# From the fourth norm to the third attention: one stage of 64 batches instead of five stages in a row

## Chip, cores, metric

One core of a Trainium2 chip runs the whole program. The metric is the device time in microseconds (us) of one execution; lower is better.

## What is computed

Eight layers act on x, 32 batches of 128 tokens with 128 features (4,096 rows). Each adds its result to x after a layer norm. The change touches layers five to seven, and the weighted addition that ends layer four:

```
x = x + _L1_ffn_ref(_layernorm(x), ...)                         # experts, two rows per token come back
x = x + _L2_xattn_ref(_layernorm(x), ctx_1024, ctx_1024, L2_xattn_w_concat)
x = x + _L2_ffn_ref(_layernorm(x), L2_ffn_weight, L2_ffn_bias)  # values rounded to float8, one 128x128 product
x = x + _L3_xattn_ref(_layernorm(x), ctx_1024, ctx_1024, L3_xattn_Wq, L3_xattn_Wk, L3_xattn_Wv, L3_xattn_Wo)

def _L2_xattn_ref(query, key, value, w_concat):      # 16 heads of 8 features
    scores = einsum('bhqd,bhkd->bhqk', q, k) / sqrt(d_k)
    ctx = einsum('bhqk,bhkd->bhqd', softmax(scores), v)
    return ctx @ w_concat.T
```

The third attention is the same with its queries, keys and values first projected by Wq, Wk and Wv. Batches do not mix: what happens to one batch of x depends on that batch and its context alone.

## The kernel before

x lies in on-chip memory as `k.X`, 32 tiles of 128 tokens by 128 features. Four tiles are a chunk (CHUNKS = 8). The program is a row of stages, each a block of its own: all engines meet at its end, and the next one begins with its memsets and loads. The stages in question are called in `network` as

```
        norm_phase(k, "n4", routed=2)
        softmax_phase(k, "a2", w_o=a["L2x_Wo"], ctx_tok=a["ctx_tok"])
        norm_phase(k, "n5", quant=(a["L2f_wT"], a["L2f_b"]))
        norm_phase(k, "n6", add_y=True)
        softmax_phase(k, "a3", *(a[f"L3x_W{w}"] for w in "qkvo"))
```

`norm_phase` (L238) works on all 32 tiles in passes. VectorE (DVE) adds the returned expert rows (L234) or the transposed result of the float8 layer (L432), takes the statistics of every tile (L442, L448), and only then are all reciprocal roots made at once (ScalarE, ACT, L338; DVE L458). DVE normalises (L468), TensorE (PE) transposes four tiles into one PSUM bank (L386), ACT copies that out (L349, L352), and DVE subtracts to get the low part (L485), so that each float32 value is held as a high and a low part. In n5 the same pass rounds to float8 and multiplies by the quantised weights (L400); n6 turns the result back (L372) and adds it.

`softmax_phase` (L2155) then treats the 32 batches one by one, a batch being an item. The queue of SyncE (SP) writes queries and keys of a chunk to DRAM (L2285, L2297) and reads them back in the layout in which four heads share a product: twelve transfers of 32 KB per two batches into `ring` (L2318), three of 256 KB per chunk into `stat` (L2331). For one item PE makes four score products (`scores`, L2423); DVE takes the row maxima of each (`top`, L2599), splits them in two parts (L2607, L2609); PE turns them (L2430), ACT puts them under the queries (`keep_max`, L2538); PE makes the shifted, transposed scores (`shifted`, L2439), ACT the exponentials (`curve`, L2545), PE the products with the values (`times_v`, L2454); the result is taken out (L2550), turned (L2464), divided (DVE L2616, L2619), turned again (L2469), multiplied by the output weights (L2473) and added to X (`add`, L2625). The order of the instructions on each engine is written out by hand in its `item`: scores of the next item, the second half of the values of the last one and its ending lie between the shifted groups of this one. There are two PSUM banks for scores and two for shifted scores, so the third score product waits for the maxima of the first. GpSimd (POOL) spreads the values of each item into `select` (L2387), two copies per item.

In a3 each item also has one of four pieces of a chunk ahead of it (`next_piece`): three 512-column products for values, keys or queries (L115 to L117, `mm3`), or the transposes of the values (L2406); POOL splits keys and queries (L2367, L2369).

## Time and profile before

| | us |
|---|---|
| device time, three runs | 2375.51, 2400.9, 2409.84 (median 2400.9) |
| profiled execution: its span | 2426.7 |
| n4, from the end of the last experts' products to a2's first instruction | 1280 to 1333 |
| a2: until its first score, then 32 items | 1333 to 1350.5, to 1581 |
| n5, n6 | 1581 to 1651.5 |
| a3: until its first score, then 32 items | 1651.5 to 1682.4, to 1902 |

The profiled execution has no time of its own beside the span, which counts from its first instruction to its last. PE is busy 1647.8 us of it (68%), DVE 1160.6, ACT 964.2, POOL 833.2. In the rows further on, times are us from the start of the span unless marked ns; PEclk is TensorE's granted clock as a share of 2.4 GHz, so 0.50 means 1.2 GHz. A busy PE is not PE at its peak: its matmuls overlap, and at the lower clock the same ones take longer.

### The profile page before, as it was taken

The page shows a single profiled execution, that of the slowest core. Times are in us where ns is not written, and L with a number is a line of the kernel's source. Part 1 is how long each engine was busy: PE and PEld are TensorE (multiplying, and loading weights), DVE is VectorE, ACT ScalarE, POOL GpSimd, SP SyncE. Part 2 cuts the span into 40 slices and gives each one's busy share as a digit, 9 for nine tenths or more (in the row PEclk, how much of TensorE's full clock was granted, in tenths as well). Part 3 has the DMA queues.
Part 4 walks back from the last instruction along what each step waited for, and adds up shares of the span by engine and source line. Part 5 has one row for each costly group of instructions (what it writes and reads, how often), then busy time and mean ns, then how long its engine had stood idle before and what let it go on. Part 6 is the DMA issues. An engine that isn't in the chain of part 4 may idle for free. (4 is left out here: it accounts for less than half of the span.)

```text
span 2426.7 us, 39580 instructions
## 1 busy us (share of the span) xinstructions
PE 1647.8 (68%) x10584; PEld 1305.3 (54%) x10584; DVE 1160.6 (48%) x3507; ACT 964.2 (40%) x2129; POOL 833.2 (34%) x994
## 2 busy tenths in 40 slices
PE   2009933989924888610991799935999626888883
PEld 2009933779913777610991577723777514555552
DVE  3302247542265777630226446675466584334463
ACT  0004412743314887400441435625466313454541
POOL 1364523855514111037450100002112047714447
PEclk9999975999956999755995558955699658999996
DMA  5727840227622333021322524202243032534432
GB/s 158 276 64 207 233 122 17 92 73 216 201 78 79 95 89 91 3 70 60 102 60 76 139 71 109 66 2 78 71 119 87 5 141 69 145 102 121 123 92 62
DMA packets 210383, 246.40 MB, mean 102 GB/s; under 512 B 36064, under 2 KB 168416, under 8 KB 208800
## 3 DMA queue, kind: packets, MB, share of 16 engines
q1 hardware_dynamic: 188832, 199.16, 29.2%
q0 software_dynamic: 21376, 45.13, 5.7%
q8 instruction: 83, 1.36, 0.2%
q14 instruction: 92, 0.75, 0.1%
HBM read 150.09 MB, written 94.10 MB: 101 GB/s over the span
## 5 line engine op out<-in xcount | busy, mean ns | idle before, releaser
L912 POOL DMA_INDIRECT out_rows<-m_yr,ids x220 | 211.2, 960 | 235.2 <-DVE ids L1096 190.1
L1039 ACT ACTIVATE m_hf<-m_psu,m_b 128x256 f32<-128x256 f32 x284 | 116.7, 470 | 361.8 <-PE m_psu L981 361.8
L524 POOL DMA_INDIRECT in_rows<-Y,sent_to x192 | 207.0, 1078 | 149.0 <-issue 57.6
L2599 DVE TENSOR_REDUCE a_mx<-a_pss 128x4 f32<-128x512 f32 x256 | 170.2, 686 | 127.8 <-PE a_pss L2423 127.7
L994 PEld LDWEIGHTS m_psy<-m_raw,m_hf 128*128 128x128 f32 x1760 | 213.4, 192 | 5.4
L981 PE MATMUL m_psu<-m_xt,m_raw 128*128 128x256 f32 x880 | 213.8, 387 | 1.8 <-DVE m_xt L1085 1.2
L994 PE MATMUL m_psy<-m_raw,m_hf 128*128 128x128 f32 x1760 | 213.8, 275 | 0.0
L2439 PEld LDWEIGHTS a_psx<-a_stat,a_ring 128*128 128x128 f32 x1024 | 182.1, 234 | 20.8 <-issue 9.4
L968 PE MATMUL m_pst<-ident,select 128*128 128x128 f32 x220 | 44.0, 283 | 205.3 <-DMA select<-in_rows 203.4
L2439 PE MATMUL a_psx<-a_stat,a_ring 128*128 128x128 f32 x1024 | 183.3, 310 | 0.1
L2545 ACT ACTIVATE Y<-a_psx 128x512 f32<-128x512 f32 x256 | 151.5, 597 | 75.6 <-PE a_psx L2439 66.7
L1306 POOL DMA_INDIRECT m_got<-out_rows,sent_to x128 | 123.8, 967 | 165.0 <-DMA out_rows<-m_yr 88.7
L981 PEld LDWEIGHTS m_psu<-m_xt,m_raw 128*128 128x128 f32 x880 | 162.5, 195 | 21.0 <-issue 2.9
L2387 POOL COPY select<-a_vx 128x64 f32<-128x64 f32 x128 | 30.2, 237 | 380.1 <-PE a_pso L2454 377.8
L1296 POOL DMA_INDIRECT in_rows<-Y,sent_to x128 | 128.2, 1001 | 63.7 <-issue 38.7
L2423 PE MATMUL a_pss<-a_ring,a_stat 96*128 96x512 f32 x256 | 128.4, 547 | 31.3 <-DMA a_stat<-stat_rows 30.3
L1586 DVE TENSOR_TENSOR m_hrow<-m_curved,m_psa 128x128 f32<-128x128 f32 x192 | 55.4, 288 | 183.9 <-ACT m_curved L1447 183.1
L968 PEld LDWEIGHTS m_pst<-ident,select 128*128 128x128 f32 x220 | 28.4, 147 | 208.6 <-DMA select<-in_rows 205.1
L1085 DVE COPY m_xt<-m_pst 128x256 f32<-128x256 f32 x110 | 45.7, 416 | 195.9 <-PE m_pst L968 195.9
L1919 PE MATMUL a_pso<-Y,select 128*128 128x128 f32 x1024 | 136.9, 280 | 0.0
L1919 PEld LDWEIGHTS a_pso<-Y,select 128*128 128x128 f32 x1024 | 133.1, 197 | 2.6
L1375 PE MATMUL m_psa<-m_experts,m_xt 128*128 x384 | 120.8, 397 | 0.6 <-ACT m_xt L1442 0.6
(330 smaller groups left out, 3549.7 us busy)
## 6 DMA issues: line engine op xcount, KB each, us to landing
m_raw<-in_L0f_w SPq DMA_DIRECT2D x41, 512.0 KB, 3.6
m_raw<-in_L0x_w SPq DMA_DIRECT2D x39, 512.0 KB
a_ring<-mov_rows SPq DMA_DIRECT2D x576, 32.0 KB
a_stat<-stat_rows SPq DMA_DIRECT2D x72, 256.0 KB, 4.2
in_rows<-xn SPq DMA_DIRECT2D x7, 2448.0 KB, 32.9
select<-in_rows SPq DMA_DIRECT2D x110, 136.0 KB
n_got<-out_rows SPq DMA_DIRECT2D x24, 512.0 KB, 4.1
m_xr<-in_rows SPq DMA_DIRECT2D x96, 128.0 KB
```

The lines of the kernel that those rows point to most:

```text
L524: pool.indirect_dma_start(k.in_rows[:], bass.IndirectOffsetOnAxis(ap=k.sent_to[:, j, i:i + 1], axis=0), rows[:, i], None).then_inc(sem, 16)
L912: pool.indirect_dma_start(k.out_rows[:], bass.IndirectOffsetOnAxis(ap=k.ids[:, n:n + 1], axis=0), yr[:, b % OUT, i], None).then_inc(y_out[ ...
L981: last = pe.matmul(psu[b % 2][:, f * B:f * B + B], raw[:, n % RAW, f * D:f * D + D], xt[:, b % 2], start=True, stop=True)
L994: last = pe.matmul(psy[b % 2][:, D * i:D * i + D], hf[:, b % 2, f * B + D * i:f * B + D * i + D], raw[:, v, UP + f * D:UP + f * D + D], st ...
L1296: pool.indirect_dma_start(k.in_rows[:], bass.IndirectOffsetOnAxis(ap=k.sent_to[:, j, i:i + 1], axis=0), k.rows[:, i], None).then_inc(sent[ ...
L1306: pool.indirect_dma_start(got[:, g % GOT], None, k.out_rows[:(h + 1) * NT * D], bass.IndirectOffsetOnAxis(ap=k.sent_to[:, j, i:i + 1], axi ...
L1375: pe.matmul(psg[n % 2], xt[:, n % 2], wres[:, bass.ds(expert[n] * WC, UP)], start=True, stop=True) \
L1919: last = pe.matmul(pso[j % 2][:, D * o:D * o + D], window, prob[:, j % 2, g, D * (h % 4):D * (h % 4) + D], start=r == 0, stop=r == OCT - 1)
L2423: pe.matmul(pss[g % 2][:], stat[:ROWS, u, g, b * D:b * D + D], ring[:ROWS, s, g, :, D * (b % 2):D * (b % 2) + D], start=True, stop=True).t ...
L2439: last = pe.matmul(psx[g % 2][:, D * h:D * h + D], ring[:, s, g, h, D * (b % 2):D * (b % 2) + D], stat[:, u, g, b * D:b * D + D], start=Tr ...
L2545: act.activation(prob[:, j % 2, g], psx[g % 2][:], ACT.Exp, scale=scale).then_inc(probs.sem, 1)
L2599: dve.tensor_reduce(mx[:, j % 2, 4 * g:4 * g + 4], pss[g % 2][:].rearrange("p (h q) -> p h q", h=4), AX.X, ALU.max).then_inc(maxed.sem, 1)
```

## The change

The five stages become one block, `stream_phase`, of 64 items: item n is batch n of the second attention for n below 32, and batch n - 32 of the third from 32 on. What the norms did in passes is done per chunk, at fixed places between the items, by a class `ChunkNorm` with three instances: `before` (norm in front of the second attention), `middle` (in front of the float8 layer), `after` (in front of the third attention). The statistics stay on DVE; the reciprocal root is now exp(-0.5 ln(v + eps)) on ACT with one refinement step in five small POOL instructions; POOL normalises; PE transposes into a bank of its own, `psn`.

```
    def normalise(self, pool, c):
        ...
        pool.wait_ge(self.rooted.sem, self.rooted.done(c))
        step(0, pool.tensor_scalar(v, self.agg[:, u, :, 1], EPS, -0.5, ALU.add, ALU.mult))
        step(1, pool.tensor_tensor(f, y, y, ALU.mult))
        step(2, pool.tensor_tensor(f, f, v, ALU.mult))
        step(3, pool.tensor_scalar(f, f, 1.5, None, ALU.add))
        step(4, pool.tensor_tensor(r, f, y, ALU.mult))
        ...
        for t in range(TPC):
            last = pool.tensor_scalar(self.xhat[:, t], self.k.X[:, cols(c * TPC + t, D)], self.agg[:, u, t, 0:1],
                                      r[:, t:t + 1], ALU.subtract, ALU.mult)
        last.then_inc(self.normed.sem, 1)
```

The first two chunks are done ahead of the items; for the others `chunk_at(n, s)` gives the chunk whose step is due in item n = 4c + s. On PE:

```
+                if (c := chunk_at(n, -6)) is not None and c >= 2:
+                    turn_norm(before, "before", c)
+                if (c := chunk_at(n, 7)) is not None:
+                    turn_norm(middle, "middle", c)
                 pe.wait_ge(max_kept.sem, max_kept.done(n))
...
+                if (c := chunk_at(n, 11)) is not None:
+                    turn_norm(after, "after", c)
+                if (c := chunk_at(n, 8)) is not None:
+                    quant_product(c)
```

DVE gets a function `aside(n, slot)`, called after each of the first three `top` of an item and at its end, with the statistics of one tile of the middle norm per item, of two tiles of the others in two items of four, the low parts (128x512, two per chunk), the cast to float8 and the addition of the float8 layer's result. ACT gets per chunk three pairs of Ln and Exp, two high parts and one rounding copy; POOL three `normalise`, one cast to float16, the bias over a chunk, and for chunks 2 to 7 `add_returned` (eight 128x128 multiplications and four 128x256 additions). The float8 product has its operands swapped, so its result needs no transpose back, and n6's turns (L336, L372) go.

The ring has three slots instead of four, `pso` one bank with both parities, and everything is unrolled, with waits on constants. The projections (`chunk_piece`) are now due from item 24 to 55. Semaphores of ended stages are used again (`k.rest`), `k.eps` is a memset more in the first stage.

In front of the first scores stand twenty products whose result nobody reads, and DVE's first maxima stand behind statistics of chunk 2:

```
+            turn_norm(before, "before", 0)
+            turn_norm(before, "before", 1)
+            pe.wait_ge(loaded.sem, loaded.done(6))
+            pe.wait_ge(wquant.sem, wquant.done(0))
+            pe.wait_ge(wl_done.sem, wl_done.done(0))
+            for _ in range(WARM):          # WARM = 20
+                pe.matmul(psr[:], k.context[:, 0, 0, :], k.context[:, :TPC, 0, :], start=True, stop=True)
+            for g in range(GROUPS):
+                scores(0, g)
+            turn_max(0)
...
+            dve.tensor_tensor(wl[:], wraw, wh[:].bitcast(F32), ALU.subtract).then_inc(wl_done.sem, 1)
+            dve.memset(ring[:ROWS, 2].rearrange("p g h q -> p (g h q)").bitcast(F32), 0.0).then_inc(slot_zeroed.sem, 1)
+            dve.wait_ge(added_rows.sem, added_rows.done(1))
+            before.statistics(dve, 2, 0, 2)
+            for g in range(GROUPS):
+                top(0, g)
```

PE at the start of the second attention. Before: psn does not exist, pss are the score banks, psm holds the turned maxima.

```order
L2393 UNCONDITIONAL_BRANCH
L2423 MATMUL a2_pss0<-a2_ring,a2_stat 128x512
L2423 MATMUL a2_pss1<-a2_ring,a2_stat 128x512
L2423 MATMUL a2_pss0<-a2_ring,a2_stat 128x512
L2423 MATMUL a2_pss1<-a2_ring,a2_stat 128x512
L2430 MATMUL a2_psm<-ident,a2_mxs 32x128
```

And after:

```order
L2570 UNCONDITIONAL_BRANCH
L2237 MATMUL a2_psn<-ident,a2_xh4 128x128 x8
L2729 MATMUL a2_psr<-context 128x512 x20
L2625 MATMUL a2_pss0<-a2_ring,a2_stat 128x512
L2625 MATMUL a2_pss1<-a2_ring,a2_stat 128x512
L2625 MATMUL a2_pss0<-a2_ring,a2_stat 128x512
L2625 MATMUL a2_pss1<-a2_ring,a2_stat 128x512
L2632 MATMUL a2_psm<-ident,a2_mxs 32x128
```

The eight transposes of the first two chunks and the twenty products have come ahead of the scores. The same place on the SP queue, after (before, it held only the load of wo, the two stores, the values and the first ring and stat):

```order
L2373 DMA a_got<-out_rows 128x4x256 x2
L2380 DMA mov_long<-context 128x4x128 x2
...
L2413 DMA a_ring<-mov_long 8x4x256 x12
L2380 DMA mov_long<-context 128x4x128 x2
L2391 DMA stat_long<-xn 128x2x512
L2423 DMA a_stat<-stat_long 32x4x512 x3
L2413 DMA a_ring<-mov_long 8x4x256 x12
L2373 DMA a_got<-out_rows 128x4x256
```

The returned rows of chunk 2 (the last row) now stand behind the first queries and behind the second twelve ring transfers. Last, PE in the middle, from the end of an item. Before:

```order
L2473 MATMUL a2_psr<-a2_wo,scratch 128x128
L2430 MATMUL a2_psm<-ident,a2_mxs 32x128
L2423 MATMUL a2_pss0<-a2_ring,a2_stat 128x512
L2423 MATMUL a2_pss1<-a2_ring,a2_stat 128x512
L2454 MATMUL a2_pso1<-Y,select 32x128 x8
```

After, at an item with n = 4c + 11:

```order
L2678 MATMUL a2_psr<-a2_wo,scratch 128x128
L2237 MATMUL a2_psn<-ident,scratch 128x128 x4
L2632 MATMUL a2_psm<-ident,a2_mxs 32x128
L2625 MATMUL a2_pss0<-a2_ring,a2_stat 128x512
L2625 MATMUL a2_pss1<-a2_ring,a2_stat 128x512
L2658 MATMUL a2_pso<-Y,select 32x128 x8
```

The four transposes of the third norm stand in line between this item's output product and the turned maxima of the next.

## Rows read from the trace of the kernel before

**Rows 1.** Windows in both attention stages: busy us, PEclk, DMA share.

```profile
1355.00:1474.00 119.00, 119.00 (x748) 88.84 (x746) 47.94 (x113) 46.51 (x89) 5.92 (x25) 0.50 0.37 96
1474.00:1572.00 98.00, 97.89 (x1068) 73.20 (x1067) 67.69 (x163) 65.61 (x127) 8.50 (x36) 1.00 0.32 85
1688.00:1737.00 49.00, 48.82 (x288) 37.17 (x287) 17.75 (x41) 20.21 (x38) 5.90 (x13) 0.50 0.39 98
```

**Rows 2.** Keep_max on ScalarE, once per item: by tile, then timeline.

```profile
L2538 ACT ACTIVATE a_stat<-a_psm x64: 589/589/590, 1355.4 to 1893.4; 32x512 fp32r<-32x512 f32 x64
...
1437.44 0.59 ACT L2538 ACTIVATE a_stat<-a_psm 32x512 fp32r<-32x512 f32 x1 [0.50 <-PE a_psm L2430]
...
1446.82 0.59 ACT L2538 ACTIVATE a_stat<-a_psm 32x512 fp32r<-32x512 f32 x1 [0.50 <-PE a_psm L2430]
...
1534.10 0.59 ACT L2538 ACTIVATE a_stat<-a_psm 32x512 fp32r<-32x512 f32 x1 [0.20 <-PE a_psm L2430]
...
1539.51 0.59 ACT L2538 ACTIVATE a_stat<-a_psm 32x512 fp32r<-32x512 f32 x1 [0.20 <-PE a_psm L2430]
...
1716.91 0.59 ACT L2538 ACTIVATE a_stat<-a_psm 32x512 fp32r<-32x512 f32 x1 [0.50 <-PE a_psm L2430]
...
1727.57 0.59 ACT L2538 ACTIVATE a_stat<-a_psm 32x512 fp32r<-32x512 f32 x1 [0.50 <-PE a_psm L2430]
...
1806.52 0.59 ACT L2538 ACTIVATE a_stat<-a_psm 32x512 fp32r<-32x512 f32 x1 [0.19 <-PE a_psm L2430]
...
1812.59 0.59 ACT L2538 ACTIVATE a_stat<-a_psm 32x512 fp32r<-32x512 f32 x1 [0.19 <-PE a_psm L2430]
```

**Rows 3.** Timeline: start of n4, first queries of a3, last addition.

```profile
1287.35 6.39 SPq L321 DMA_DIRECT2D n_got<-out_rows  x3
...
1291.16 2.98 DVE L234 SCALAR_TENSOR_TENSOR X<-n_got,gates,X 128x128 f32<-128x128 f32 x11 [14.71 <-DMA n_got<-out_rows]
...
1673.37 0.42 SPq L2285 DMA_DIRECT2D stat_rows<-xn  x1
1676.60 1.27 SPq L2331 DMA_DIRECT2D a_stat<-stat_rows  x3
1678.12 5.00 SPq L2318 DMA_DIRECT2D a_ring<-mov_rows  x12
...
1682.41 1.19 PE L2423 MATMUL a_pss<-a_ring,a_stat 96*128 96x512 f32 x2 [9.82 <-DMA a_stat<-stat_rows]
...
1901.49 0.29 DVE L2625 TENSOR_TENSOR X<-X,a_psr 128x128 f32<-128x128 f32 x1 [1.27 <-PE a_psr L2473]
```

**Rows 4.** Timeline of TensorE in a3: 512-column products, four transposes at either clock.

```profile
1657.59 0.63 PE L116 MATMUL a_psm<-context,a_wh 128*128 128x512 f32 x1
1658.02 0.63 PE L117 MATMUL a_psm<-context,a_wl 128*128 128x512 f32 x1
...
1664.48 1.12 PE L2406 MATMUL a_psm<-ident,scratch 128*128 128x128 f32 x4 [1.17 <-ACT scratch L2533]
...
1783.52 0.66 PE L2406 MATMUL a_psm<-ident,scratch 128*128 128x128 f32 x4
```

**Rows 5.** Groups by line, VectorE, 1265 to 1925: busy us, mean ns.

```profile
L442 DVE BATCH_NORM_STATS2 n_bst<-X 128x6 f32<-128x128 f32 x128 | 26.2, 278 | 3.6 <-DMA n_br<-in_L3f_rb 3.6
...
L485 DVE TENSOR_TENSOR xn<-n_xs,xn 128x512 fp32r<-128x512 f32 x19 | 12.5, 694 | 1.8 <-ACT xn L352 1.8
```

**Rows 6.** Groups by line, GpSimd, and L409 (ns min, median, max).

```profile
L2387 POOL COPY select<-a_vx 128x64 f32<-128x64 f32 x128 | 30.2, 237 | 380.1 <-PE a_pso L2454 377.8 <-issue 2.1 <-DMA a_vx<-in_ctx_tok 0.3
...
L2369 POOL TENSOR_TENSOR context<-scratch,context 128x512 f32 x4 | 5.1, 1280 | 0.7 <-POOL context L2367 0.7
...
L409 POOL TENSOR_TENSOR X<-X,Y x8: 1292/1310/2259, 371.6 to 387.9; 128x512 f32<-128x512 f32 x8
```

**Rows 7.** Windows in the last stage, around a pause of TensorE.

```profile
2360.00:2364.00 4.00, 0.93 (x7) 0.70 (x6) 2.65 (x8) 1.11 (x2) 2.99 (x4) 0.99 0.27 74
2364.00:2367.00 3.00, 3.00 (x8) 2.32 (x8) 1.66 (x4) 0.00 (x0) 2.18 (x3) 0.50 0.39 104
```

More of the change, by code:

```diff
@@ L2272, in softmax_phase @@
+        mov_rows, stat_rows = k.mov_long, k.stat_long
         by_head = mov_rows.rearrange("(g r i) c -> r i g c", r=4, i=HD)
@@ L2401, in chunk_piece, with norm_bank, turn_norm @@
-            def chunk_piece(i, u, q):
-                c, n = chunk(i, u), piece(i, u, q)
-                pe.wait_ge(piece_out.sem, piece_out.free(n))
+            held = []
+            def norm_bank():
+                if held:
+                    kind, c = held.pop()
+                    for s in {"before": (high4, low4), "after": (high6, low6), "middle": (eighth,),
+                              "quant": (rounded,)}[kind]:
+                        pe.wait_ge(s.sem, s.done(c))
+            def turn_norm(norm, kind, c):
+                norm_bank()
+                norm.turn(pe, c, psn)
+                held.append((kind, c))
@@ new lines, in quant_product, with chunk_piece @@
+            def quant_product(c):
+                norm_bank()
+                pe.wait_ge(half_x.sem, half_x.done(c))
+                for t in range(TPC):
+                    last = pe.matmul(psn[:, D * t:D * t + D], x16[:, D * t:D * t + D], wq[:], start=True, stop=True,
+                                     skip_group_check=True)
+                last.then_inc(product.sem, 1)
+                held.append(("quant", c))
+            def chunk_piece(n):
+                if next_piece(n) is None:
+                    return
+                C, q = next_piece(n)
+                c, m = C - CHUNKS, piece(C, q)
+                if m >= 1:
+                    pe.wait_ge(piece_out.sem, piece_out.done(m - 1))
@@ L2484, in item, with turn, out @@
-            def item(i, j, more, behind, first):
+            def turn(n):
+                pe.wait_ge(onorm.sem, onorm.done(n))
+                pe.transpose(psr[:, :D], ost[:, n % 2], k.ident[:]).then_inc(oturned.sem, 1)
+            def out(n):
+                pe.wait_ge(otaken.sem, otaken.done(n))
+                pe.matmul(psr[:, D:2 * D], ot[:, n % 2], wo[:, n // TILES], start=True, stop=True,
+                          skip_group_check=True).then_inc(oproj.sem, 1)
+            def item(n):
+                more, behind = n + 1 < ITEMS, n > 0
@@ new lines, in item @@
+            def item(n):
+                more, behind = n + 1 < ITEMS, n > 0
+                if behind:
+                    take_raw(n - 1)
+                chunk_piece(n)
+                curve(n, 0)
+                if (c := chunk_at(n, -6)) is not None and c >= 2:
+                    high(before, high4, c)
+                curve(n, 1)
+                curve(n, 2)
+                if (c := chunk_at(n, 5)) is not None:
+                    middle.inverse_root(act, c)
+                if (c := chunk_at(n, 10)) is not None:
+                    after.inverse_root(act, c)
```

870 lines of the change are left out of this document (552 added, 318 removed).

## Prediction

> **What bounds the kernel now.** I read the 25-us windows over the five stages first, then the repetition of one instruction that comes once per item, then the starts of the stages, then the groups by line.
>
> In both attention stages TensorE is the engine that never rests: 119.00 of 119 us, 97.89 of 98, 48.82 of 49 [rows 1]. But it does so at two speeds. From 1355 to 1474 it has granted clock 0.50 and gets through 748 matmul records; from 1474 to 1572 it has 1.00 and gets through 1068 in less time. The period of an item shows the price: 1446.82 - 1437.44 = 9.38 us at 1.2 GHz, 1539.51 - 1534.10 = 5.41 at 2.4 GHz in the second attention; 10.66 and 6.07 in the third, with its projections [rows 2]. So 119 us held some 13 slow items, and the 49 us from 1688 with the 6 us before the next rise hold some 6. At the high clock DVE is busy 67.69 of 98 us, 3.7 per item, ACT 65.61 and POOL 8.50 [rows 1]: there is room beside TensorE, most of all on POOL. What is left of the 614 us from 1287.35 to 1901.49 [rows 3] goes to the norms and stage starts, in which no item runs: up to the first keep_max at 1355.4, and the 101 us between a2's end at 1581 and a3's first score at 1682.4 [rows 3]. The 64 keep_max start between 1355.4 and 1893.4 [rows 2], 538 us for 63 intervals.
>
> **Part 1: the stage start.** The new stage starts where n4 did, at 1287.35, with the returned rows in DVE's hands at 1291.16 [rows 3]. Chunk 0 then passes DVE (eight additions at 2.98/11 = 0.27 us [rows 3], statistics four times 0.28 [rows 5], their merging about half of that), ACT (two small instructions, about 0.5), POOL (nine instructions), PE (four transposes, 1.12 [rows 4]), ACT's copy (0.59, as keep_max's 512 columns [rows 2]) and DVE's low part (0.69 [rows 5]). POOL never did a tensor_scalar here: its copy of half as many elements takes 0.24, a quarter of its 512-column two-input instruction 0.32 [rows 6], and the worst of L409 a quarter of 2.26, 0.56. I take 0.3 for 128x128 and 0.25 for the small ones with their waits, so 2.5 for a `normalise`, bounds 1.6 to 3.5. Sum: low part of chunk 0 ready near 1301; call this T.
>
> SP stores the queries at T; in a3 the fetch followed the store by 1676.60 - 1673.37 = 3.2 us, and the first score came 1682.41 - 1676.60 = 5.8 later [rows 3]. So scores could start at T + 9. DVE's first maximum cannot: it stands behind the statistics of chunk 2, those behind POOL's `add_returned`, and that behind a transfer issued after the queries (3 issues, 1.5) and twelve ring transfers (5.0 [rows 3]), so at T + 10. It lands 3.8 to 5.8 later [rows 3]; four multiplications and two 256-column additions are 2.5 (to 3.5), the statistics 0.9. First maximum: T + 17 to T + 20, I take 1320.5. The four maxima, the split, the turn and keep_max follow as in a2, where keep_max came 4.9 after the first score at 1350.5, some 4.2 after the first maximum began: first keep_max at 1324.7 instead of 1355.4, 31 us gained.
>
> **Part 2: the 101 us in the middle go.** Nothing waits for a whole X any more: the first item of the third attention comes one period after the last of the second. SP's chain for the next chunk's queries has about three items' time, as it had in a3, and three ring slots are still two pairs ahead.
>
> **Part 3: what the items now carry.** Per chunk PE has three groups of four transposes at 0.66 (1.12 at the low clock) [rows 4] and four float16 products, which I put at the same 0.5: 2.5 us in four items, 0.6 each. At the high clock that makes 6.0 from 5.41. DVE's extra per four items, with all norms running: ten to twelve tiles of statistics at 0.28 + 0.15, two low parts 1.4, the cast 0.4 and the addition 0.6, about 7.2, so 3.7 + 1.8 = 5.5 per item. Both engines being that full, and taking turns, I put 6.2 for items 0 to 23. From 24 to 39 the projections come on top while the first norm is done: 6.07 + 0.5 = 6.6. From 40 to 55: 6.07. The last eight: 5.41. POOL's load is three normalises 7.5, `add_returned` 5, spreading 2, cast and bias 2: 17 us in a time of 25; its splits take the place of `add_returned` later. PE waits in line for POOL's normalise of the third norm in the same item (second piece of the order shown); I take nothing for it, and up to 1 us per four items as a bound. 24 x 6.2 + 16 x 6.6 + 15 x 6.07 + 8 x 5.41 = 389 us for 63 intervals, and 1901.49 - 1893.4 = 8.1 after the last [rows 2, 3].
>
> Everything at the high clock, the stage ends at 1324.7 + 389 + 8.1 = 1722: 180 us earlier than 1901.5. This is the sum before the clock is asked.
>
> The Trainium skill, "SBUF — State Buffer", section "Who interferes with whom", says that VectorE instructions with two on-chip inputs and GpSimd hold one port pair in turns. Rows agree that far as one L409 took 2.26 against 1.29. By that rule single POOL instructions grow by what DVE's take; DVE's are mostly with a PSUM input, so it changes nothing in the sum but leans to the upper bound for POOL.
>
> **Part 4: do the twenty products hold the clock up?** They start when DVE has split the weights: chunk 1 has gone the way of chunk 0 (some 5.5 us behind it), and the weights take two instructions of 384 columns, 1.0 to 1.5 by L485's 0.69 for 512 [rows 5], so near T + 7. A 512-column product follows the last by 1658.02 - 1657.59 = 0.43 at the low clock [rows 4] and by half of that at the high one, so they end between T + 12 and T + 16. I expect them to raise the clock. But then PE has two score products, and must wait for the first maximum at T + 17 to 20; after it the scores come one per 0.7, the time of a maximum. The nearest case in the trace: PE busy 0.93 of 4 us, and the clock, still 0.99 in that stretch, is 0.50 in the next, where PE is busy 3.00 of 3.00 [rows 7]. A pause of some 4 us followed by thin work is what stands here. So my forecast is that the clock falls back before the first items, and that these run at 1.2 GHz as in a2 and a3.
>
> How long? A dense stream alone did not raise it for 13 items in a2 and for 6 in a3. The three timed runs lie 17 to 51 us below the profiled span; if that is all slow items at 4 us, they had 7 to 15 in both stages together. I take 8 for the one stage. Each costs 9.38 + 0.7 - 6.2 = 3.9 us: 31 us.
>
> Sum: -180 + 31 = -149; 2426.7 - 149 = 2278, I say 2280. Against the median of 2400.9 that is 5% less; since part of what the median lacks to the span is the same slow items, I subtract nothing more.
>
> The Trainium skill, "TensorE: Matmul & The Clock Gate", section "HAM oscillation — how this bites in real kernels", has the clock full as long as PE works without long pauses. By that rule every item runs at 5.41 to 6.6 soon after the first ones, and the time would be that of rival A. The 119 us of rows 1, busy throughout at 0.50, speak against it.
>
> **Rivals.**
> A. The high clock holds from the first item: the first maximum comes earlier than I reckon, or the four score products are enough. For it: scores, turned maxima and two more scores follow each other; against it the wait above. 2426.7 - 180 = 2247.
> B. The clock rises late, with the projections from item 24 on or after: some 30 slow items, 24 x 3.9 + 6 x 4.75 = 122 of the 180 given back: 2369. For it: a2 alone needed 13 items, and norm transposes are no denser than the work they interrupt.
> C. Waits in line: PE behind POOL's normalise, DVE behind PE's transposes, POOL at its upper bounds (25 to 28 us of work per four items). A us and a half more in 40 items: 60 us, 2340.
> D. Slower than before: the low clock holds for the whole stage, since every norm step breaks the stream. 24 x 10.1 + 16 x 11.4 + 15 x 10.66 + 8 x 9.38 = 660 instead of 389, so +91: 2518. It decides from 42 slow items on (24 x 3.9 + 18 x 4.7 = 178). Against it: both stages rose within 13 items.
>
> **How the numbers follow.** Forecast (falls back, rises within 3 to 15 items): 0.58, time 2280, its own range 2260 to 2310. A 0.18, B 0.10, C 0.09, D 0.05. The range 2235 to 2350 takes in A and C and leaves out most of B, D and an A with cheaper norms. A measurement tells about 2% from no change; 2% below 2400.9 is 2353, which in this sum is reached with fewer than 27 slow items. Faster by over 2%: 0.87; within 2%: 0.08 (B); slower: 0.05 (D).
>
> **What would show it.** The first item's ACT instruction near 1325, periods of about 10 at clock 0.50 and then 6.0 to 6.6 at 1.00; the clock at 1.00 during the last of the twenty products and 0.50 right after; no hole at the 33rd item; POOL busy some 65% in the first half. Wrong would be: clock 1.00 from the first item (A), periods over 7 at the high clock with PE waiting for `psn` transposes (C), a clock that falls again within the 64 items, or a first maximum before T + 14, which would undo the reason for the fall.

## The result, and the profile after

The changed kernel takes 2288.8 us, median of four runs (2274.01, 2287.77, 2289.78, 2296.46); the kernel before, on the same chip, 2405.4 (2375.51, 2400.9, 2409.84, 2420.72). The ratio is 0.9539, 95% interval 0.945 to 0.9627: 4.6% faster. Forecast were 2280 us and a range of 2235 to 2350. The profiled execution of the changed kernel took 2274.01 us with a span of 2272.3, against the span of 2426.7 before, 154.4 less. By the medians it is 116.6 less: the profile before is longer than all four timed runs of that kernel, the one after is the fastest of its four. On the chips of the experiments further on, the kernel before takes 2507.4 to 2626.4 us, and the ratios there count only its runs within 1.5% of its fastest, 2 of 11 on the last chip; against the median of all eleven, 2588.4, the changed kernel's 2408.3 would be 7% less.

Busy time of the whole span, from the page of the changed kernel (before: PE 1647.8, DVE 1160.6, ACT 964.2, POOL 833.2; so TensorE is busy for 72 us less and idle for 83 us less, and GpSimd has 144 us more to do):

```profile
PE 1576.2 (69%) x10596; PEld 1260.3 (55%) x10596; DVE 1101.3 (48%) x3313; ACT 930.5 (41%) x2133; POOL 976.8 (43%) x1293
```

The repetition of ScalarE's keep_max (line 2770 now, 2538 before), once per item, by tile, as in [rows 2]:

```profile
L2770 ACT ACTIVATE a_stat<-a_psm x64: 589/589/590, 1315.7 to 1739.9; 32x512 fp32r<-32x512 f32 x64
```

All 64 items now stand in one run from 1315.7 to 1739.9 us, 424 us for 63 intervals; before it was 538 us, with 101 us of norms in the middle. The windows (us, then busy us and records of PE, PE's weight loads, DVE, ACT, POOL; granted clock, DMA share, GB/s), to be laid beside [rows 1]:

```profile
1305.00:1312.00 7.00, 3.86 (x16) 2.77 (x14) 2.19 (x6) 0.00 (x0) 4.97 (x9) 0.97 0.77 227
1312.00:1316.00 4.00, 2.35 (x5) 1.15 (x6) 2.62 (x6) 0.28 (x1) 2.93 (x6) 0.53 0.99 266
1316.00:1336.00 20.00, 19.15 (x118) 14.03 (x118) 8.98 (x23) 11.21 (x17) 5.36 (x14) 0.50 0.29 76
1336.00:1397.00 61.00, 55.62 (x593) 41.76 (x591) 48.33 (x140) 38.88 (x82) 44.14 (x94) 1.00 0.45 130
1397.00:1442.00 45.00, 43.70 (x276) 32.49 (x276) 22.58 (x68) 18.60 (x39) 29.41 (x59) 0.51 0.28 81
1442.00:1466.00 24.00, 21.79 (x236) 16.47 (x228) 20.10 (x62) 15.92 (x35) 17.12 (x39) 1.00 0.39 110
1466.00:1479.00 13.00, 10.54 (x66) 7.99 (x67) 5.11 (x17) 4.22 (x8) 8.48 (x14) 0.50 0.53 134
1479.00:1746.00 267.00, 259.94 (x2715) 196.60 (x2712) 177.46 (x463) 181.68 (x366) 98.14 (x215) 1.00 0.34 91
```

The clock is 0.50 until 1305.5, 3.5 us into the twenty products (1301.96 to 1308.40), then 1.00 to 1312.3, 0.50 to 1336.2, 1.00 for 61 us, and it falls twice more, at 1397.6 for 44 us and at 1465.9 for 14. At either clock the items do what [rows 1] showed: 43.70 of 45 us busy with 276 records at the low clock, 259.94 of 267 us with 2715 at the high one. From 1479.5 to the end it stays up.

The start of the stage, timeline (start, us, engine, line, operation; in brackets the idle time ahead and what ended it), where [rows 3] has the old one:

```profile
1288.23 3.14 POOL L2230 TENSOR_SCALAR a_xh<-X,na_agg,na_rstd 128x128 f32<-128x128 f32 x4
...
1291.43 1.12 PE L2237 MATMUL a_psn<-ident,a_xh 128*128 128x128 f32 x4 [24.47 <-POOL a_xh L2230]
...
1293.21 0.69 DVE L2875 TENSOR_TENSOR xn<-a_psn,xn 128x512 fp32r<-128x512 f32 x1 [3.95 <-ACT xn L2748]
...
1301.96 6.44 PE L2729 MATMUL a_psr<-context 128*128 128x512 f32 x20 [2.36 <-DVE a_wl L2956]
...
1306.87 2.34 POOL L2511 TENSOR_SCALAR a_got<-a_got,gates 128x128 f32<-128x128 f32 x4 [8.51 <-DMA a_got<-out_rows]
...
1308.23 0.63 PE L2625 MATMUL a_pss<-a_ring,a_stat 96*128 96x512 f32 x2
1309.30 1.52 POOL L2516 TENSOR_TENSOR X<-X,a_got 128x256 f32<-128x256 f32 x2
...
1310.85 0.48 DVE L2194 BATCH_NORM_STATS2 na_bst<-X 128x6 f32<-128x128 f32 x2 [4.77 <-POOL X L2516]
...
1311.54 1.25 DVE L2844 TENSOR_REDUCE a_mx<-a_pss 128x4 f32<-128x512 f32 x2
...
1312.25 1.39 PE L2625 MATMUL a_pss<-a_ring,a_stat 96*128 96x512 f32 x2 [3.38 <-DVE a_mx L2844]
...
1315.72 0.59 ACT L2770 ACTIVATE a_stat<-a_psm 32x512 fp32r<-32x512 f32 x1 [11.85 <-PE a_psm L2632]
```

SP's first issue of the stage is at 1278.18. Chunk 0's low part is ready at 1293.90, 15.7 us later (forecast 13.6). The products run from T + 8.1 to T + 14.5; two scores follow, and then TensorE idles for 3.38 us until VectorE's first maximum at T + 17.6, which stands behind the statistics of chunk 2, and these behind GpSimd's additions. First keep_max 37.5 us after the stage's start (forecast 37.3).

The first of the later falls, at item 11. GpSimd's timeline around it:

```profile
1384.58 0.20 POOL L2222 TENSOR_SCALAR nb_var<-nb_agg 128x4 f32<-128x4 f32 x1
...
1386.04 3.13 POOL L2230 TENSOR_SCALAR scratch<-X,nb_agg,nb_rstd 128x128 f32<-128x128 f32 x4
1389.16 2.34 POOL L2511 TENSOR_SCALAR a_got<-a_got,gates 128x128 f32<-128x128 f32 x4
1391.58 1.53 POOL L2516 TENSOR_TENSOR X<-X,a_got 128x256 f32<-128x256 f32 x2
...
1393.56 0.19 POOL L2222 TENSOR_SCALAR nc_var<-nc_agg 128x4 f32<-128x4 f32 x1
...
1395.02 3.13 POOL L2230 TENSOR_SCALAR scratch<-X,nc_agg,nc_rstd 128x128 f32<-128x128 f32 x4
1398.13 2.34 POOL L2511 TENSOR_SCALAR a_got<-a_got,gates 128x128 f32<-128x128 f32 x4
```

And TensorE's of the same time:

```profile
1393.35 0.65 PE L2658 MATMUL a_pso<-Y,select 128*32 128x128 f32 x16 [0.57 <-POOL select L2536]
...
1395.14 0.49 PE L2678 MATMUL a_psr<-a_wo,scratch 128*128 128x128 f32 x2
1398.30 1.08 PE L2237 MATMUL a_psn<-ident,scratch 128*128 128x128 f32 x4 [2.67 <-POOL scratch L2230]
```

GpSimd works with no gap above 0.1 us from the normalise of the second norm at 1384.58 through additions at 1389.16 to the normalise of the third norm, whose four instructions end at 1398.15. TensorE waits in line for them from 1395.6 on, 2.67 us, and 2.0 us into this wait, at 1397.6, the clock falls to 0.50.

The second of the later falls looks alike in a list of waits, but its order in time is another. TensorE's timeline:

```profile
1463.52 0.64 PE L2658 MATMUL a_pso<-Y,select 128*32 128x128 f32 x16 [0.57 <-POOL select L2536]
1464.61 0.33 PE L2674 MATMUL a_psr<-ident,scratch 128*128 128x128 f32 x1 [0.45 <-DVE scratch L2865]
...
1468.46 1.09 PE L2237 MATMUL a_psn<-ident,scratch 128*128 128x128 f32 x4 [2.67 <-POOL scratch L2230]
```

The clock falls at 1465.88, the wait of 2.67 us begins at 1465.79. What lies ahead of the fall is a row of short waits: from 1462.5 to 1465.9 TensorE is busy for 2.27 of 3.4 us.

Groups by line inside the stage, GpSimd (busy us, mean ns):

```profile
L2511 POOL TENSOR_SCALAR a_got<-a_got,gates 128x128 f32<-128x128 f32 x48 | 28.1, 602 | 8.5 <-DMA a_got<-out_rows 8.5
...
L2230 POOL TENSOR_SCALAR scratch<-X,nc_agg,nc_rstd 128x128 f32<-128x128 f32 x32 | 25.1, 794 | 0.9
...
L2516 POOL TENSOR_TENSOR X<-X,a_got 128x256 f32<-128x256 f32 x24 | 17.4, 725 | 1.9
```

A 128x128 tensor_scalar with two values per row takes 0.79 us on GpSimd, one with one value 0.60, where the prediction took 0.3, an estimate from other instructions in [rows 6].

### The profile page after: what moved, and what is told of

The parts are those of the page before. It is cut to its first block and busy times, and to the rows that moved or that the text cites. A ratio compares the mean times of both kernels' runs of the same rounds, so it can differ in the third digit from the quotient of the medians.

```text
span 2272.3 us, 37352 instructions
## 1 busy us (share of the span) xinstructions
PE 1576.2 (69%) x10596; PEld 1260.3 (55%) x10596; DVE 1101.3 (48%) x3313; ACT 930.5 (41%) x2133; POOL 976.8 (43%) x1293
## 5 line engine op out<-in xcount | busy, mean ns | idle before, releaser
L538 POOL DMA_INDIRECT in_rows<-Y,sent_to x192 | 198.2, 1032 | 149.3 <-issue 57.6
L2642 PEld LDWEIGHTS a_psx<-a_stat,a_ring 128*128 128x128 f32 x1024 | 162.6, 210 | 14.2 <-issue 4.6
L2642 PE MATMUL a_psx<-a_stat,a_ring 128*128 128x128 f32 x1024 | 163.8, 286 | 0.1
L1310 POOL DMA_INDIRECT in_rows<-Y,sent_to x128 | 127.9, 1000 | 63.7 <-issue 38.7
L1119 DVE TENSOR_TENSOR m_yr<-m_psy,m_b 128x256 f32<-128x256 f32 x71 | 30.1, 424 | 186.8 <-PE m_psy L1008 186.8
L2625 PE MATMUL a_pss<-a_ring,a_stat 96*128 96x512 f32 x256 | 115.3, 493 | 3.4 <-DVE a_mx L2844 3.4
```

The costliest lines, as they stand in the source:

```text
L538: pool.indirect_dma_start(k.in_rows[:], bass.IndirectOffsetOnAxis(ap=k.sent_to[:, j, i:i + 1], axis=0), rows[:, i], None).then_inc(sem, 16)
L1310: pool.indirect_dma_start(k.in_rows[:], bass.IndirectOffsetOnAxis(ap=k.sent_to[:, j, i:i + 1], axis=0), k.rows[:, i], None).then_inc(sent[ ...
L2642: last = pe.matmul(psx[g % 2][:, D * h:D * h + D], ring[:, s, g, h, D * (n % 2):D * (n % 2) + D], stat[:, C % 2, g, b * D:b * D + D], star ...
```

## The experiments

Twelve kernels on three other chips: eleven edits of the changed kernel, and that kernel itself. The first four rows below the top one share a chip, the next four a second, the last four a third. On those chips the kernel before has medians of 2577 to 2615 us, and the changed kernel itself 2408. The stage is not where the chips differ (470.0 us in e_nowarm, 469.8 in the profile above). So I compare kernels by their traces of this stage, and whole times only on one chip. "Low" in the table is the time at granted clock 0.50 between the first and last keep_max; "stage" is from SP's first issue of the stage to the start of its last addition.

| kernel | low, us | 63 intervals, us | stage, us | median (runs) | ratio to before |
|---|---|---|---|---|---|
| changed kernel, profile above | 78 | 424.1 | 469.8 | 2288.8 (4) | 0.954 |
| e_nowarm | 78 | 424.2 | 470.0 | 2423.5 (4) | 0.956 |
| e_first_max | 140 | 444.9 | 487.7 | 2426.6 (4) | 0.956 |
| e_turn_later | 83 | 425.5 | 471.3 | 2418.0 (4) | 0.955 |
| e_both | 116 | 437.8 | 481.4 | 2422.4 (4) | 0.951 |
| e_add_dve | 95 | 429.8 | 472.4 | 2389.9 (4) | 0.951 |
| e_fill_start | 106 | 437.5 | 483.3 | 2427.8 (4) | 0.963 |
| e_fill_norm | 25 | 413.0 | 458.6 | 2403.2 (4) | 0.956 |
| e_add_fill | 51 | 416.6 | 462.0 | 2399.6 (4) | 0.952 |
| e_own_fill | 85 | 423.5 | 469.8 | 2406.0 (6) | 0.953 |
| e_all | 3.4 | 396.2 | 439.2 | 2378.2 (6) | 0.943 |
| e_all_unfilled | 28 | 405.3 | 448.0 | 2384.5 (6) | 0.945 |
| e_same (the changed kernel) | 118 | 438.9 | 484.3 | 2408.3 (6) | 0.956 |

The intervals of the ratios are 0.004 to 0.02 wide to either side, since the kernel before varies so much; no two rows of the last column can be told apart by them, except e_fill_start (0.9591 to 0.9665), the dearest, from e_all (0.9346 to 0.9511) and e_all_unfilled (to 0.9532). What can be told apart are the traces, and on one chip the times of some kernels: all four runs of e_add_dve (2385.91 to 2415.81) lie below those of e_fill_start (2418.40 to 2430.91).

Each trace is one execution, and executions of one kernel vary: the changed kernel has 78 us of low clock in one and 118 in another. These two, executions of one program, give the price of the low clock: (438.9 - 424.1) / (117.6 - 78.5) = 0.38 us lost per us. With e_all, in which edits are contained too, it comes out the same: (438.9 - 396.2) / (117.6 - 3.4) = 0.37.

**The products alone.**

```diff
-    WARM = 20
+    WARM = 0
```

> The changed kernel without its twenty unread products, nothing else touched. My theory (the clock rises with the products and is lost again in the 3.4 us in which TensorE waits for the first maximum, so they buy nothing): granted clock 0.50 from the first item on, first keep_max within 1 us of 37.5 us after the stage start, a slow stretch of the same 3 to 4 items, time within 6 us of the changed kernel's 2289. Rival (the products shorten the slow stretch though the clock falls after them): 6 to 13 slow items instead of 3, each 3.5 us dearer, so 10 to 35 us slower, 2299 to 2324.

Measured: granted clock 0.50 through the start, first keep_max 37.7 us after the stage's start, then the same periods to 0.1 us as with the products (7.1, 10.4, 7.4, 6.0 ...), stage 470.0 against 469.8. So in this form of the kernel the twenty products buy nothing. The windows of e_nowarm, in which TensorE is busy for 1.19 of the 9 us before the first maximum and the clock then rises as late after the first keep_max as it does with the products:

```profile
1301.00:1311.00 10.00, 1.66 (x7) 0.89 (x5) 3.43 (x9) 3.30 (x5) 4.15 (x9) 0.50 0.59 159
1311.00:1320.00 9.00, 1.19 (x2) 0.50 (x2) 3.64 (x2) 1.89 (x1) 3.99 (x7) 0.50 0.76 201
1320.00:1345.00 25.00, 21.54 (x123) 15.21 (x124) 12.55 (x33) 11.49 (x17) 9.29 (x22) 0.50 0.43 113
```

**The first maximum earlier.** VectorE's wait for chunk 2's rows and their statistics move behind `split_max(0)`.

```diff
-            dve.wait_ge(added_rows.sem, added_rows.done(1))
-            before.statistics(dve, 2, 0, 2)
             for g in range(GROUPS):
                 top(0, g)
             split_max(0)
+            dve.wait_ge(added_rows.sem, added_rows.done(1))
+            before.statistics(dve, 2, 0, 2)
```

> VectorE takes the first four maxima before, not after, it waits for chunk 2's added rows. My theory: TensorE's idle time behind the products shrinks from 3.4 us to under 1.5, the clock stays at 1.00 into the items, the first three items take 6.2 us instead of 7.1, 10.4 and 7.4; with the 2.6 us that the first maximum comes earlier 9 us less, 2280. Later falls stay as they are. Rival (the clock falls anyway, as scores and maxima take turns and TensorE has little to do until the first item runs): slow first items as before, at most 2.6 us less, 2286.

Measured: the maximum comes right behind the first scores, the first keep_max 2.9 us earlier in the stage, and the clock falls all the same, at 1316.9. The rival held. TensorE's timeline of e_first_max shows why the cure was too small:

```profile
1309.54 2.95 PE L2729 MATMUL a_psr<-context 128*128 128x512 f32 x11
1312.33 0.63 PE L2625 MATMUL a_pss<-a_ring,a_stat 96*128 96x512 f32 x2
1313.50 1.09 PE L2625 MATMUL a_pss<-a_ring,a_stat 96*128 96x512 f32 x2 [0.55 <-DVE a_mx L2844]
1315.98 0.41 PE L2632 MATMUL a_psm<-ident,a_mxs 128*32 128x128 f32 x2 [1.39 <-DVE a_mxs L2854]
```

The 3.38 us have become three holes of 0.55, 0.1 and 1.39 us within 3.0. The cause that I had named, one wait of TensorE, was only a part of the thin stretch between products and first item.

**The third norm's transposes half an item later**, with ScalarE's and VectorE's parts of them.

```diff
                 shifted(n, 1)
+                if (c := chunk_at(n, 12)) is not None:
+                    turn_norm(after, "after", c)
...
                 shifted(n, 3)
...
-                if (c := chunk_at(n, 11)) is not None:
-                    turn_norm(after, "after", c)
```

> TensorE's four transposes for the third norm, ScalarE's copy and VectorE's low part of them stand half an item later, so that TensorE no longer waits in line for GpSimd's normalise of the same item. My theory: the items of 8.2 and 7.4 us at the high clock (every fourth from item 23 to 39) become 6.2 to 6.5, some 8 us in all, and the clock does not fall at the items near 11 and 19, 7 slow items at 3.5 to 4.5 us, 28 us: together 36 less, 2253. First rival (the falls have another cause than that wait): only the 8 us, 2281, clock 0.50 in two stretches as before. Second rival (GpSimd itself is full, the wait only moves to the next thing that TensorE or VectorE takes from it): no gain, 2289, and waits for GpSimd under another name.

Measured: three falls behind the start, stage 471.3. The items of 8.2 us are gone, but a group of four costs 6.5 + 7.0 + 6.3 + 6.2 where it cost 5.6 + 6.3 + 6.2 + 8.2: 26.0 and 26.3. The second rival held. The waits of TensorE in e_turn_later (us in total, times, longest):

```profile
PE a_pso L2658 <- POOL select L2536: 10.4, 5, 3.1
```

Two rows of its timeline:

```profile
1406.27 1.08 PE L2658 MATMUL a_pso<-Y,select 128*32 128x128 f32 x16 [3.09 <-POOL select L2536]
...
1440.29 1.08 PE L2658 MATMUL a_pso<-Y,select 128*32 128x128 f32 x16 [3.10 <-POOL select L2536]
```

TensorE now waits for GpSimd's `select` copies of the next item, which stand behind the same normalise. The clock falls inside each of these holes, at 1405.4 and 1439.5, and in a third at 1473.7. GpSimd is late; which instruction of it TensorE meets is secondary. Both edits together:

> Both edits: first maxima before chunk 2's rows, and the third norm's transposes half an item later. My theory: clock 1.00 from the products to the end of the stage, 45 us less than the changed kernel, 2244. Rival (one of the two causes is wrong): 2253 if only the later falls go, 2280 if only the first does, 2281 if none does and only the wait is gone.

Measured: 116 us of low clock, stage 481.4. The first low stretch lasts 58 us, and three falls follow. Neither cause had been removed.

**GpSimd relieved.** VectorE adds the returned rows of chunks 2 to 7, eight instructions a chunk.

```diff
+            def add_returned(c, first):
...
+                    for t in range(first, first + 2):
+                        i = c * TPC + t
+                        last = dve.scalar_tensor_tensor(k.X[:, cols(i, D)], got[:, c % 2, t, cols(j, D)],
+                                                        k.gates[:, j, i:i + 1], k.X[:, cols(i, D)], ALU.mult, ALU.add)
+                    last.then_inc(added_rows.sem, 1)
...
-                    add_returned(c, 0)
```

> The additions of the returned rows, chunks 2 to 7, by VectorE (eight instructions of some 0.3 us a chunk) in place of GpSimd's 7.7 us a chunk. Theory now: in items 8 to 23 GpSimd's queue is the one that runs late, TensorE waits for it, and in those holes the clock falls. Then GpSimd's share in the first 24 items goes from 72% to some 45%, TensorE's waits for it go from 9.9 us to under 2, the clock does not fall after it has risen, and items 8 to 23 take 6.2 us: stage 470 us after its first issue becomes 470 - 7 slow items x 4 - 5 of waits - 2.5 for the earlier first maximum = 434. Rival (the falls have nothing to do with GpSimd's lateness): slow stretches remain, 460 to 485. Second rival (VectorE, 79% busy, becomes the bound): high clock, but periods of 6.8 and more in items 4 to 23.

Measured: the first low stretch lasts 75 us instead of 24, yet the later falls shrink to 17 and 3.4 us, and the longest wait for the third norm's rows from 2.7 to 1.1 us. At the high clock the groups of items 8 to 19 take 6.3 + 6.3 + 6.8 + 7.4 = 26.8 us. The theory held for its own place, and the total, 472.4 instead of 434, was eaten by a first stretch that nothing in the edit explains. It need not be typical: the profiled run, 2415.81 us, is the slowest of four, and the others take 2385.91 to 2392.22. If they differ from it in this stage alone, their stage takes some 443 to 449 us, an estimate; there is no trace of them.

**The holes filled with unread products**, at the start and ahead of the third norm's transposes.

```diff
+                if n == 0:
+                    for _ in range(3):
+                        pe.matmul(psr[:], k.context[:, 0, 0, :], k.context[:, :TPC, 0, :], start=True, stop=True)
...
+            unread(WARM)
+            scores(0, 0)
+            scores(0, 1)
+            unread(16)
+            scores(0, 2)
+            unread(2)
+            scores(0, 3)
+            unread(6)
             turn_max(0)
```

> Unread products not only ahead of the first scores but in every gap up to the first item: 16 more between the second and third score, 2, 6 and 3 at the next waits, some 6 us at the high clock. Theory: it is the thin stretch between the products and the first item in which the clock falls; filled, it stays at 1.00 through the first three items, 7.1, 10.4 and 7.4 us become three of 6.0 to 6.3, 6 us less for the stage (470 to 464), later falls unchanged in kind. Rival (the clock falls whatever TensorE does there, and rises again some 24 us later): the three periods stay and the stage takes 470 or, by the products themselves, up to 3 us more.

Measured: clock 1.00 from 1307.5 to 1328.0, item 0 in 5.1 us; then it falls for 48 us, and the stage takes 483.3. Neither theory nor rival: the start held, and a second hole stood behind it, which in the changed kernel is only 0.85 us long, since TensorE is at the low clock there and comes to it later. TensorE's timeline in e_fill_start:

```profile
1327.84 0.59 PE L2669 MATMUL a_psr<-ident,scratch 128*128 128x128 f32 x2 [2.95 <-ACT scratch L2795]
```

And ScalarE's in the changed kernel, which has the same instructions:

```profile
1324.03 3.61 ACT L2741 ACTIVATE a_ring<-a_own 32x4096 fp32r<-32x4096 f32 x1
1327.67 0.38 ACT L2784 ACTIVATE scratch<-a_pso 128x256 f32<-128x256 f32 x1
```

TensorE waits 2.95 us for ScalarE, which copies the own rows into the third ring slot (3.61 us) before it takes item 0's output.

```diff
                 norm_bank()
+                if kind == "after":
+                    for _ in range(8):
+                        pe.matmul(psn[:], k.context[:, 0, 0, :], k.context[:, :TPC, 0, :], start=True, stop=True)
                 norm.turn(pe, c, psn)
```

> Eight unread products into the free bank ahead of each wait for the third norm's rows, 8 x 0.22 = 1.8 us at the high clock, where TensorE waits up to 2.7 us. Theory: the hole in TensorE's stream is what lets the clock fall; filled, the clock stays at 1.00 from the first rise on, 7 slow items x 4 = 28 us less, and where there was no wait the products cost 1.8 us in up to 5 chunks, 9: stage 470 becomes 451. Rival (not the hole but the state of the whole stretch): slow stretches stay, and with 8 x 1.8 to 3.5 us for the products the stage takes 480 to 490.

Measured: after the first rise the clock stays at 1.00 but for 3.4 us, and the stage takes 458.6. Items 11, 15 and 19 take 10.3, 10.3 and 10.9 us, 4 more than their neighbours: at the first of these the eight products take 2.09 us and TensorE still waits 0.79 us for GpSimd behind them. So the products shorten nothing; they fill the wait, and the long falls are gone with it. This holds for three of the four runs: 2400.03 to 2404.26 us at a mean clock over the whole program of 0.852 to 0.853. The fourth takes 2426.35 at 0.836; it was low for longer somewhere, and where is not on record. Windows of e_fill_norm, beside the 61, 45, 24 and 13 us of the changed kernel above:

```profile
1344.00:1460.00 116.00, 105.55 (x1103) 78.77 (x1102) 89.18 (x265) 72.26 (x155) 88.98 (x187) 1.00 0.42 120
1464.00:1743.00 279.00, 274.78 (x2820) 208.41 (x2818) 183.28 (x480) 186.26 (x374) 104.31 (x225) 1.00 0.35 92
```

> The additions on VectorE and the filled start together. Theory: clock 1.00 from the products to the last item, stage 434 - 6 = 428 us, the whole 5 to 7% under the kernel before. Rivals as for the two alone: 455 to 470 if only one of them holds the clock.

Measured for the two together: 462.0 us, one low stretch of 48 us from the hole behind ScalarE's copy (again 2.95 us, up to 1330.89) and one of 3.4.

**All holes of the start.** The own rows' copy for slot 2 goes ahead of the first keep_max, into ScalarE's 11.85 idle us; start filled.

```diff
             own_rows(1)
+            own_rows(2)
             keep_max(0)
...
-                if n == 0:
-                    own_rows(2)
```

> As the filled start, and ScalarE's copy of the own rows into the third ring slot (3.61 us) stands ahead of the first keep_max, where ScalarE is idle for 11 us, instead of behind item 0, where TensorE waited 2.95 us for the copy of item 0's output behind it. Theory: those were the two holes of the start, and the clock was lost in the second once the first was filled; now it stays at 1.00 from the products to item 11, first periods 5.1, 6 and 6, then the falls at items 11 to 19 as before: 470 - 3 x 3.5 - 3 = 457 for the stage. Rival (the clock falls at the start whatever the holes): slow stretch of 3 to 7 items in the first ten, 470 to 485.

Measured: clock 1.00 from 1315.3 to 1397.2, first periods 5.1, 5.3, 6.1. With both holes filled or moved away the clock holds through the start; with only the first filled (e_fill_start, e_add_fill) it did not. The stage still takes 469.8, since the fall at item 11 now lasts 85 us. Windows of e_own_fill:

```profile
1316.00:1397.00 81.00, 75.53 (x749) 56.88 (x747) 60.65 (x173) 47.02 (x98) 56.46 (x120) 1.00 0.50 139
1397.00:1482.00 85.00, 83.56 (x520) 62.70 (x524) 43.91 (x129) 36.05 (x76) 53.60 (x108) 0.50 0.27 77
1483.00:1755.00 272.00, 263.87 (x2754) 199.73 (x2753) 181.82 (x477) 184.59 (x371) 100.14 (x218) 1.00 0.36 94
```

**Everything together**: that, additions on VectorE, and five unread products ahead of the third norm's transposes for chunks 0 to 3; then the same without any product at the start (the three ahead of item 0 go as well); then the changed kernel itself.

```diff
-            unread(16)
+            unread(6)
...
+                if kind == "after" and c < 4:
+                    for _ in range(5):
+                        pe.matmul(psn[:], k.context[:, 0, 0, :], k.context[:, :TPC, 0, :], start=True, stop=True)
```

> Start filled (20, 6, 2, 6 and 3 products) and the own rows early, additions on VectorE, and five unread products ahead of the third norm's transposes of chunks 0 to 3. Theory (every fall of the clock follows a hole in TensorE's stream of some 2 us or more): clock 1.00 from the products to the last item, sum of the 63 intervals 24 x 6.5 + 16 x 6.6 + 15 x 6.0 + 8 x 5.4 = 395 us, stage 37 + 395 + 8 = 440, that is 30 less than the changed kernel on the same chip, 1.3%. Rival (low stretches come without a hole too): one or two of them, 450 to 465.

```diff
-            unread(WARM)
...
-            unread(6)
...
-            unread(2)
...
-            unread(6)
```

> The same without any unread product at the start, the twenty of the change among them. Theory (with the holes of the start gone the products have a worth at last): clock 0.50 from the first item for 3 to 8 items, stage 12 to 30 us longer than with them, 452 to 470. Rival (the clock rises by itself within an item or two once the stream has no hole): within 5 us of it.

> The changed kernel itself, as a yardstick on this chip. Stage 470 us, ratio to the kernel before as on record within its interval, 0.945 to 0.963. A rival reading of the record (the clock's pattern in the first profile was an accident of one execution) wants another pattern of slow items and a stage of under 460 or over 480.

Windows of e_all:

```profile
1315.00:1502.00 187.00, 175.39 (x1781) 132.05 (x1780) 155.65 (x465) 117.51 (x247) 97.02 (x221) 1.00 0.45 124
1502.00:1505.00 3.00, 3.00 (x23) 1.74 (x24) 1.94 (x5) 1.57 (x3) 2.28 (x5) 0.56 0.13 48
1505.00:1727.00 222.00, 216.10 (x2247) 163.70 (x2245) 141.74 (x362) 149.84 (x297) 67.71 (x148) 1.00 0.35 93
```

e_all's stage takes 439.2 us, 440 expected. Its six runs lie between 2376.88 and 2382.36, those of the changed kernel on the same chip between 2403.80 and 2431.18: by the medians 1.25% less, and no run of one reaches the other. The mean granted clock over the whole program is 0.854 to 0.856 in e_all's six runs and 0.830 to 0.845 in those of the changed kernel, so the gain is not that of the profiled run alone. The one fall in the profile, 3.4 us long, follows a wait of 1.11 us for the third norm's rows of a chunk past the filled ones. Without the products at the start there are 28 us of low clock instead of 3.4, and the stage takes 448.0, 8.8 more; the medians differ by 6.3 us, with runs that overlap a little (2378.85 to 2391.45, of which the profiled one is the slowest). That lies between the 12 of the theory and the 5 of the rival: with the holes gone the start's products have a worth, of about 0.3%. e_same had the pattern of the first profile up to item 10, then low stretches of 10 and 85 us, and a stage of 484.3: the rival held, and the pattern behind item 10 is a draw. Of its six runs two, the profiled one among them, take 2428 and 2431 us, the other four 2404 to 2409. e_all changes four things at once; how its 30 us divide among them is not shown.

**All pauses and falls together.** In the thirteen profiles (the first and the twelve) TensorE paused 21 times for 2.5 to 3.4 us between its first scores and the last item, each time entering the pause with the clock at 1.00 or within 0.1 us of its fall. All 21 have a fall of the clock close by. In 18 it comes 1.3 to 4.2 us after the pause began. In the other three it comes at the very beginning, 0.09 us into the pause in the changed kernel (1465.88, shown above), 0.11 us in e_nowarm (1474.90) and 0.05 us ahead of it in e_fill_start (1409.91), so that these pauses cannot have been its cause. Of 27 pauses of 0.9 to 1.1 us behind the start, 5 have a fall, each 3.4 us long. Four falls behind the start have no pause over 0.8 us near them (3.4, 6.8, 17 and 34 us long). So a long pause at the high clock is always near a fall here, mostly ahead of it, but pauses are not its only way down, and my sentence "every fall follows a hole of some 2 us or more" was too strong.

## Why the prediction was right, point by point

**Part 1, the start.** The first keep_max came 37.5 us after the stage's start, 37.3 forecast, with errors that offset each other, so the match is luck. GpSimd's normalise takes 4.7 us (1286.65 to 1291.37), not 2.5 and outside the bounds of 1.6 to 3.5, which makes T 2.1 us later than forecast; and an addition of two tiles takes 3.9 us, not 2.5. But SP's issue of chunk 2's rows came at T + 8.3, not T + 10, and of the range T + 17 to T + 20 the forecast took 19.5, where 17.6 was measured.

**Part 2, the middle.** Held, no gap at the 33rd item: its keep_max comes 7.9 us after the 32nd, and the next 6.0 later; 7.9 to 8.2 us is what every fourth item takes there.

**Part 3, the items.** At the high clock items 24 to 39 take 105.4 / 16 = 6.59 (6.6 forecast), items 40 to 54 6.03 (6.07), the last eight intervals 5.56 (5.41). Items 0 to 23 were put at 6.2: in e_all, where they run at the high clock, they take 154.0 / 24 = 6.42, unread products included. The tail is 8.1 (8.1). What failed is the sentence "I take nothing for it, and up to 1 us per four items as a bound" on the wait behind the third norm's normalise. The wait is 2.67 us in items 11 and 19. The reason is the sum for GpSimd just ahead, 17 us of work per four items: by the trace it is 13.9 for three normalises, 7.7 for the additions, 1.9 for spreading and 1.9 for the cast and the bias, 25.4 in all, as much as four items last; in items 12 to 15 GpSimd is busy for 25.6 us. With this wait and shorter ones the groups of items 8 to 19 take 28.5, 29.0 and 29.5 us at the high clock (e_fill_norm), where 24.8 were forecast. So rival C was present with some 12 us. Beyond this the wait opened a hole of the next part.

**Part 4, the clock.** Forecast: the products raise the clock, it falls in the wait for the first maximum, eight slow items, 31 us. The rise, the wait and the fall are in the rows. e_nowarm shows that the products were then worth nothing, e_own_fill that the clock holds once TensorE has no hole between them and item 1. But the wait named was one of several, as e_first_max showed, and the next one, behind ScalarE's 3.61 us, was not in the text. The size of the loss came out right, though it was made of other parts: 78.5 us of low clock x 0.37 = 29 us, 20.5 us of it at the start and 58 in two later falls, the event that the text listed as wrong, "a clock that falls again within the 64 items".

The Trainium skill, "TensorE: Matmul & The Clock Gate", section "HAM oscillation — how this bites in real kernels", describes a clock that is lost in each pause of TensorE between groups of products. That a fall can come in such a pause this case's traces confirm, with pauses of 2.67 us at item 11 and 3.1 us in e_turn_later. By its rule, no long pauses and a full clock, the low stretch of e_own_fill should not have lasted: TensorE was busy for 83.56 of 85 us, all at 0.50, and the measurement decides.

**The sum.** Against the profiled spans: forecast 149 less, measured 154.4. The stage itself, from its first issue to its last addition, went from 614.1 us [rows 3] to 469.8, 144.3 less. Of the other 10, 9.2 lie in front of it (it starts at 1278.18 instead of 1287.35) and 0.9 behind it, in stages that the change leaves as they were; the forecast has no term for them, and they are luck. In the median, for which 2280 was said, the kernel is at 2288.8: the sum started from a profile that is slower than all timed runs, and subtracted nothing for it.

Of the 144.3, 30.5 come from the start (first keep_max 68.0 us after the stage's first issue before, 37.5 now) and 108.0 from the middle (115.9 us between the 32nd and the 33rd keep_max, 7.9 now). The items themselves give only 5.9, and that is two large terms against each other: before, they ran for 172 us at 0.50, which by the periods in [rows 2] (9.38 against 5.41) cost 0.42 us per us, 73 us in all, an estimate; now 29. So some 44 us less are lost to the clock, and some 38 us of norm work have come into the items.

Rival A (no low clock) would have been some 29 us lower; nearest to it is e_all, whose stage takes 439.2 us. B and D are excluded by the rise at item 3 and the 267 us at 1.00 at the end.

## What to carry to other kernels

Once stages are merged, the engine with slack in the share of busy time can be the one that is late: count its queue item by item, with the durations of just the instruction forms that it will run, ahead of trusting a mean of 72% (44.14 of the 61 us from 1336). Unread products keep a clock only if no pause follows them; find every pause up to the dense part, also those on other engines' queues, and move work out of them first, then fill what is left. And where the clock's pattern changes between executions, read the period at each level and the low time separately: the time is the one plus 0.37 us per us of the other here. A single profile is one draw: lay the times and the mean clock of the other runs beside it before a stretch in it is explained.

## What the runs showed of the hardware that was not expected

- After a fall in a pause of 2.7 to 3.1 us behind the start the clock stayed low for 6.8 to 85 us; in [rows 7], with a pause of 3.07 us, it was back at 1.00 after 3.4 us. TensorE was busy for 43.70 of 45 and 83.56 of 85 us in two of these stretches. What ends one no run here shows; that stays open, and with it most of the spread of the kernel's time.
- A 128x128 tensor_scalar on GpSimd takes 0.60 us with one value per row and 0.79 with two, while a cast of 128x512 takes 0.61 and a 128x4 instruction 0.2. VectorE does the same instruction with two values per row (L468 of the kernel before) in 0.35. The Trainium skill, "GPSIMD Engine Reference", section "Engine selection", has instructions with two tensor inputs about twice as slow on GpSimd as on VectorE and calls those with one "roughly line-rate". For operands per row the measurement differs: 0.79 against 0.35 us.
- The pattern of slow items is the same to 0.1 us in two executions on different chips (the profile on record and e_nowarm, one with and one without the products), and different in two executions of one kernel (that profile and e_same).

Not tried: a cheaper normalise on GpSimd itself, and two of the norms on ScalarE, which is busy for 38.88 us of the 61 from 1336 to 1397.
